# Second weights kept in SBUF for the last 23 single tiles, and the leftover routing cut into one piece a pair

## Chip, cores and metric

The kernel runs on one core of a Trainium2 chip. The metric is the device time of one execution in microseconds; the profiled execution has a span of its own, which is some 2 us shorter than its device time.

## The reference

Cross attention with residual, then a routed feed-forward layer with residual, all in float32. B = 32 samples of 112 rows by 256 (3584 rows), 16 heads of 64, a context of 375 rows by 192 a sample; 8 experts of 256 x 1024 (gate and up) and 512 x 256 (down), two experts a row.

```python
x = x + _L0_xattn_ref(_layernorm(x, axis=-1), ctx_768, Wq, Wkv, Wproj, bproj)
x = x + _L0_ffn_ref(_layernorm(x, axis=-1), gate_w, gate_up_w, down_w)
...
top_k_probs, top_k_idx = jax.lax.top_k(router_probs, TOP_K)
hidden = jax.nn.silu(gate_out) * up_out
expert_out = jnp.einsum('enf,efd->end', hidden, down_w)
output = jnp.sum(sel * top_k_probs[:, :, None], axis=1)
```

Products are made as three passes of split float32 (high by high, high by low, low by high), so each operand has a rounded part (`_h`) and a rest (`_l`).

## The kernel before, in words

The program is one block of five engine programs that meet by semaphores alone. There is no scheduler: each engine runs its instructions in the order in which they are written, and one that waits holds back all behind it on that engine.

**Attention and routing** take the first 1140 us or so, sample by sample. Each row is normalised and written twice, once for each chosen expert, into `bins` in DRAM: 8 experts with a region each, in tiles of 128 rows. The last two samples are routed late, inside the expert stage.

**Expert stage.** There are `NT` = 63 tiles of 128 rows. The first `N1` = 38 are taken as `PAIRS` = 19 pairs, two tiles of one expert that share its weights; the other 25 (tiles 38 to 62) are single tiles, whose rows and experts are known only when the last two samples are routed. `over_tiles` lays out both: before, pairs 0 to 7 written out, a hardware loop (`Fori`) for pairs 8 to 17 (8 to 15 on SP), then pair 18, tiles 38 and 39, a loop over groups of four single tiles, and the last ones written out. `known(p)` is true where p is a plain number, so in written-out code.

A **pair** on TensorE (PE) is 72 products of 256 columns and four transposes: the down product of the pair before, the transposes of the next pair's rows (L1906), the second half of gate and up, and the first half of the next pair's. ScalarE (ACT) and VectorE (DVE) evacuate, split high and low parts (`pairT_h`/`pairT_l`, `hid_h`/`hid_l`), and copy the part of the gate and up weights in use into `still`. The routing of samples B-2 and B-1 is hung on the ends of pair bodies on DVE: `choose`, `mark`, `assign`, then the plan of the single tiles (`tiles_left`, `experts_left`, `rows_left`), which writes `tile_row` and `tile_expert`.

A **single tile** t on PE, between one transpose of rows (L1898) and the next: rows of t+1 turned, the hidden values of t-1 turned (L2016), up of t, gate of t+1, down of t-1. ACT: `hT_h`, `hidT_h`, `silu`, the high part of the down weights of t (L1074), and `y_out` of t-1 (L1082). DVE: `hT_l`, `hidT_l`, `dest_now` and `share_now`, the product of silu and up (L1622, into `in_fours`), the low part of the down weights (L1511). GpSimd (POOL) adds `y_out` into `out` with an indirect DMA (L869); it starts that of t-1 only when that of t-2 has landed, since both can hit one row. SyncE (SP) loads the rows of t+4 (L616) and the down weights of t+2 (L625, 512 KB into one of the two slots of `Wd`), both after the addition of t-1 has landed:

```python
sp.wait_ge(y_store[(k + 1) % 2], 16 * (2 * i + (k - 1) // 2 + 1))
...
load_rows(t + 4, k)
...
load_down(expert_of(t + 2), (k + 1) % 2, "(p k)")
```

With "(p k)" a partition gets four neighbouring rows of the down weights in one run, so the product of silu and up is written in steps of four. With "(k p)" it gets four rows 128 apart.

Of the kernel before, what the change touches and what calls it, by code (L numbers as in the profile page):

```python
# [32 lines left out]
P = 128  # L33
# [26 lines left out]
N2 = NT - N1  # L60

# [127 lines left out]
def over_tiles(eng, pair_of_tiles, tile, end=PAIRS // 2, last=NT // 4):  # L189

    for i in range(4):
        for m in range(2):
            pair_of_tiles(i, m)
    with eng.Fori(4, end) as i:
        for m in range(2):
            pair_of_tiles(i, m)
    for i in range(end, PAIRS // 2):
        for m in range(2):
            pair_of_tiles(i, m)
    pair_of_tiles(PAIRS // 2, 0)  # L200
    for k in (2, 3):
        tile(PAIRS // 2, k)
    with eng.Fori(PAIRS // 2 + 1, last) as i:
        for k in range(4):
            tile(i, k)
    for i in range(last, NT // 4 + 1):
        for k in range(4):
            tile(i, k)
# [12 lines left out]
def attention_and_experts(nc, x, ctx_in, Wq, Wkv, Wproj, bproj, gate_w, gate_up_w, down_w, out):  # L221
# [4 lines left out]
    with ExitStack() as stack:  # L226
# [119 lines left out]
        Wd = sb("Wd", [P, 2, FJ, C], F32)  # L346
# [24 lines left out]
        in_fours = nc.alloc_sbuf_tensor_at("in_fours", [P, FJ, P], F32, offset=still_at)  # L371
# [10 lines left out]
        down_parts = [down_even, sb("down_odd", [P, 2, FJ, C], F32R)]  # L382
# [65 lines left out]
        wd_in = [sem("wd_in0"), sem("wd_in1")]  # L448
# [42 lines left out]
        def _(sp):  # L491
# [131 lines left out]
            def load_down(e, slot, rows="(k p)"):  # L623

                sp.dma_start(Wd[:, slot], down_w[bass.ds(e, 1)].rearrange(f"o {rows} n -> p (o k) n", p=P)).then_inc(wd_in[slot], 16)  # L625

            def pair_of_tiles(i, m):
                p, t = 2 * i + m, 4 * i + 2 * m
                if known(p) and p == 1:
                    sp.wait_ge(x2_done, B)  # L630
                    sp.dma_start(dram_at(tokens, B - 1), x2[:, 1, :]).then_inc(x2_out[1], 16)
                if known(p) and p == PAIRS - 2:
# [10 lines left out]
                if known(p) and p >= PAIRS - 2:  # L643
                    load_down(expert_of(N1 + p - PAIRS + 2), m, "(p k)")
                else:
                    load_down(expert_of(t + 4), m)
# [24 lines left out]
            for p in range(2):  # L671
                load_down(expert_of(2 * p), p)
            over_tiles(sp, pair_of_tiles, tile, PAIRS // 2 - 1, NT // 4 - 1)
# [6 lines left out]
        def _(pool):  # L680
# [181 lines left out]
            norm_h(B - 1, 1, NP - 1)  # L862
# [20 lines left out]
            def pair_of_tiles(i, m):  # L883
# [3 lines left out]
                if known(p) and p == 4:  # L887
                    scatter(B - 2, 0, None)
                if known(p) and p == 7:
# [16 lines left out]
        def _(act):  # L906
# [164 lines left out]
            def hi_of_down(slot, landed):  # L1071

                act.wait_ge(wd_in[slot], 16 * landed)
                nc.scalar.copy(down_parts[slot][:, 0], Wd[:, slot]).then_inc(wd_hi, 1)  # L1074
# [20 lines left out]
            def pair_of_tiles(i, m):  # L1095
# [5 lines left out]
                if there(p - 1, PAIRS):  # L1101
                    for r in range(2):
                        output(t - 2 + r, (2 * m + 2 + r) % 4, pair_down[r], 2 * i + m - 1)
# [4 lines left out]
                hi_of_hidden(p, 0)  # L1108
                silu_of_pair(p, 1)
                if there(p + 1, PAIRS):  # L1110
                    hold_still(e, 1, 0)
                    if not known(p) or p >= 1:
                        act.wait_ge(down_made, t)
                    hi_of_down(1 - m, i + m + 1)
# [9 lines left out]
                if known(p) and p == 4:  # L1124
                    open_gates(B - 1, C_ps)

            def tile(i, k):
# [7 lines left out]
                if there(t, NT):  # L1135
# [6 lines left out]
                    act.wait_ge(down_made, t - 2 if known(t) and t == N1 else t - 1)  # L1142
# [913 lines left out]
```

## Time and profile before

| | us |
|---|---|
| median of 3 runs | 1502.94 (1501.08 to 1502.97) |
| the profiled execution, device time | 1502.86 |
| its span | 1501.1 |
| PE busy | 1424.6 (95%) |
| DVE, ACT, POOL busy | 1060.7, 881.0, 630.0 |
| granted TensorE clock, mean | 0.99 |

The page's table of groups is headed by the attention stage and its share of busy time is an average over all stages. The change is in the last 360 us, so the views below are of that stretch: times in them are counted from the span's start.

### The profile page before, as it was taken

Reading aid. Unit: us, or ns where it says so; the run is one execution under the profiler, and the core shown is the slowest. Engines: PE = TensorE matmul, PEld = TensorE weight load, DVE = VectorE, ACT = ScalarE, POOL = GpSimd, SP = SyncE. Lnnn points to the kernel's source line nnn. Section 1 sums busy time; section 2 is a strip of 40 time slices with the busy share of each in tenths; the row PEclk is TensorE's granted clock in tenths of the full one; section 3 lists DMA queues with packets and bytes.
Section 4 is the critical chain, followed back from the end, with each engine's and each line's share of the span. In section 5 each row is a group of like instructions: output and inputs, shape, how many; then the busy total and the mean of one; then the engine's idle time right before and its main releaser. Section 6 shows DMA issues by size and latency. Waiting matters only on the chain. (4 is left out here: it accounts for less than half of the span.)

```text
span 1501.1 us, 39049 instructions
## 1 busy us (share of the span) xinstructions
PE 1424.6 (95%) x12264; PEld 1272.7 (85%) x12265; DVE 1060.7 (71%) x2906; ACT 881.0 (59%) x2429; POOL 630.0 (42%) x671
## 2 busy tenths in 40 slices
PE   6999999999999999999999999999987999997775
PEld 5888988888888988898888888888877989986664
DVE  5667777777777777777777777777768776654543
ACT  5565655665666665655665665655657767743342
POOL 3634435454435444444544344534373433322222
PEclk9999999999999999999999999999998999999998
DMA  9322222222222222222222232111136555544443
GB/s 269 95 67 69 78 66 74 66 72 72 88 80 89 72 66 73 71 72 69 72 66 79 79 99 78 37 44 33 47 127 218 117 117 120 117 105 115 113 118 85
DMA packets 112077, 134.78 MB, mean 90 GB/s; under 512 B 17980, under 2 KB 95532, under 8 KB 111916
## 3 DMA queue, kind: packets, MB, share of 16 engines
q1 hardware_dynamic: 98860, 115.17, 26.1%
q0 software_dynamic: 12144, 15.66, 5.8%
q10 hardware_dynamic: 1024, 3.34, 0.7%
q8 instruction: 25, 0.41, 0.1%
q14 instruction: 24, 0.20, 0.0%
HBM read 81.16 MB, written 51.93 MB: 89 GB/s over the span
## 5 line engine op out<-in xcount | busy, mean ns | idle before, releaser
L963 ACT ACTIVATE prob<-bank,neg_max 112x375 f32<-112x375 f32 x512 | 300.4, 590 | 133.9 <-DVE neg_max L1429 133.9
L1429 DVE TENSOR_REDUCE neg_max<-bank 112x1 f32<-112x375 f32 x512 | 243.7, 538 | 14.7 <-PE bank L1737 14.6
L1747 PE MATMUL bank<-ident,prob 112*125 112x112 f32 x1536 | 213.8, 273 | 2.7 <-ACT prob L963 2.6
L1747 PEld LDWEIGHTS bank<-ident,prob 112*125 112x125 f32 x1536 | 198.1, 188 | 16.4 <-ACT prob L963 4.8
L869 POOL DMA_INDIRECT out<-y_out,dest_now x63 | 102.1, 1620 | 226.4 <-ACT y_out L1082 202.0
L1771 PEld LDWEIGHTS bank<-probT,V 125*64 125x64 f32 x3072 | 148.1, 137 | 39.1 <-issue 36.4
L1193 DVE TENSOR_TENSOR K_l<-bank,K_h 128x376 fp32r<-128x376 f32 x256 | 140.3, 549 | 56.8 <-ACT K_h L919 52.6
L1771 PE MATMUL bank<-probT,V 125*64 125x112 f32 x3072 | 175.5, 263 | 2.6 <-DVE probT L1435 1.8
L917 ACT COPY V<-bank 125x512 f32<-125x512 f32 x96 | 56.4, 587 | 168.1 <-PE bank L1709 165.5
L919 ACT CAST K_h<-bank 128x376 fp32r<-128x376 f32 x256 | 121.0, 473 | 30.9 <-PE bank L1702 29.3
L798 POOL TENSOR_SCALAR std<-mv 112x1 f32<-112x1 f32 x32 | 7.7, 240 | 283.4 <-DVE mv L1279 283.4
L763 POOL CAST OT_h<-O_now 128x448 fp32r<-128x448 f32 x64 | 37.3, 583 | 209.4 <-DVE O_now L1262 209.4
L969 ACT COPY probT<-bank 125x336 f32<-125x336 f32 x256 | 101.7, 442 | 38.6 <-PE bank L1747 37.7
L1183 DVE COPY V<-bank 125x512 f32<-125x512 f32 x96 | 66.4, 691 | 81.7 <-PE bank L1709 78.7
L1435 DVE COPY probT<-bank 125x336 f32<-125x336 f32 x256 | 123.7, 494 | 0.1
L1645 PE MATMUL bank<-pairT_h,still 128*128 128x256 f32 x608 | 115.6, 286 | 5.8 <-DVE pairT_l L1498 4.2
L1702 PE MATMUL bank<-yA_h,WkH 128*128 128x376 f32 x256 | 99.5, 389 | 12.4 <-DVE WkU L1211 12.4
L963 ACT ACTIVATION_READ_ACCUMULATOR prob<-bank,neg_max 112x1 f32 x512 | 108.4, 212 | 0.0
L1645 PEld LDWEIGHTS bank<-pairT_h,still 128*128 128x128 f32 x608 | 96.3, 191 | 7.2 <-DVE pairT_l L1498 5.2
L1645 PE MATMUL bank<-Wgu,hT_h 128*128 x200 | 68.9, 426 | 32.2 <-DVE hT_l L1504 32.2
L1702 PE MATMUL bank<-WvH,yA_h 128*125 128x512 f32 x192 | 90.9, 474 | 0.0
L921 ACT CAST q_h<-bank 128x224 fp32r<-128x224 f32 x128 | 45.6, 356 | 74.1 <-PE bank L1645 74.1
(244 smaller groups left out, 4128.4 us busy)
## 6 DMA issues: line engine op xcount, KB each, us to landing
bins<-pad_rows SPq DMA_DIRECT2D x29, 1032.0 KB, 5.8
Wd<-in_L_ffn_down_w SPq DMA_DIRECT2D x44, 512.0 KB
inv_rows<-sums SPq DMA_DIRECT2D x126, 128.0 KB, 2.9
h_in<-bins SPq DMA_DIRECT2D x63, 129.0 KB
Wgu<-in_L_ffn_gate_up_w SPq DMA_DIRECT2D x6, 1024.0 KB, 5.6
y_sb<-in_ctx SPq DMA_DIRECT2D x32, 187.5 KB, 2.7
y_sb<-in_ctx SPq DMA_DIRECT2D x62, 93.8 KB, 2.8
x_sb<-in_x SPq DMA_DIRECT2D x16, 224.0 KB, 2.9
```

The costliest lines, as they stand in the source:

```text
L869: pool.indirect_dma_start(out, bass.IndirectOffsetOnAxis(ap=dest_now[:, slot:slot + 1], axis=0), y_out[:, slot % 2, :], None, compute_op=A ...
L919: nc.scalar.copy(K_h[:, arg, :], src[:, 0:LKE]).then_inc(hi_done, 1)
L963: nc.scalar.activation(prob[:, j, :], S_ps[j][0:LQ, 0:LKV], ACT.Exp, bias=neg_max[:, j:j + 1], accum_out=row_sum[:, head // HB, head % HB: ...
L969: nc.scalar.copy(probT[:, j, :], S_ps[j][0:KR, 0:KT * LQ]).then_inc(probT_second, 1)
L1183: nc.vector.tensor_copy(V[:, t, half * 512:half * 512 + 512], src[0:KR, :]).then_inc(v_second, 1)
L1193: nc.vector.tensor_tensor(lo, ps, hi.bitcast(F32), ALU.subtract).then_inc(lo_done, 1)
L1429: nc.vector.tensor_reduce(neg_max[:, j:j + 1], S_ps[j][0:LQ, 0:LKV], AX.X, ALU.max, negate=True).then_inc(max_done, 1)
L1435: nc.vector.tensor_copy(probT[:, j, :], S_ps[j][0:KR, 0:KT * LQ]).then_inc(probT_first, 1)
L1645: last = mm(dst, w, m, start=n == 0, stop=n == len(todo) - 1)
L1702: last = mm(out, w, y, start=begins and n == 0, stop=ends and n == "both")
L1747: last = nc.tensor.transpose(S_ps[j][0:KR, t * LQ:t * LQ + LQ], prob[:, j, t * KR:t * KR + KR], ident[0:LQ, 0:LQ])
L1771: last = mm(O_ps[r * DK:r * DK + DK, c:c + LQ], V[:, t, (2 * p + r) * DK:(2 * p + r) * DK + DK], probT[:, 2 * k + r, t * LQ:t * LQ + LQ], ...
```

## The change

**Single tiles.** From tile 40 (`HELD`) on no down weights are loaded. Four DMAs of 1 MB (`keep_down`) put those of all eight experts into `Wd_all`, which lies over `Wd`, `still` and other tiles of the pair stage; so they are issued only as these come free: experts 0 and 1 in pair 15, 2 and 3 at the start of pair 18's part, 6 and 7 and then 4 and 5 at its end. ACT and DVE read the slice of their tile's expert from `Wd_all` by a register. From load 16 (`LATER`) on, the pairs' weights go to another place, `Wd_later`. SP waits no longer for the addition of t-1, since that wait was there for the slot of `Wd`. The odd slot of the split weights lies elsewhere (`down_third`), and the product of silu and up is written in order.

**Routing.** All 19 pairs are written out. The pieces of the last two samples' routing stand in pairs 1 to 5 and 7 to 12 instead of 1 to 7, each with less in it.

**Order in a pair.** ACT makes `y_out` of the second tile two steps later; DVE copies `dest_now` and `share_now` after the low parts. The residual of the last sample and the first split of down weights stand in the middle of pair 0, and POOL normalises the last sample after the first additions.

```diff
+LATER = 16
+HELD = N1 + 2
...
+        Wd_later = nc.alloc_sbuf_tensor_at("Wd_later", [P, 2, FJ, C], F32, offset=plan2_at)
+        Wd_all = nc.alloc_sbuf_tensor_at("Wd_all", [P, E, FJ, C], F32, offset=wd_at)
...
+            def keep_down(first):
+
+                sp.dma_start(Wd_all[:, first:first + 2].rearrange("p e k n -> p (e k) n"),
+                             down_w[first:first + 2].rearrange("e (k p) n -> p (e k) n", p=P)).then_inc(wd_all, 16)
...
+                if p == PAIRS - 1:
+                    sp.wait_ge(up_made, 2 * PAIRS - 1)
+                    keep_down(2)
                 sp.wait_ge(hT_made, t + 2)
                 sp.wait_ge(dest_done, t + 2)
...
+                load_down(p + 2, t + 4 if p + 2 < PAIRS else N1 + p + 2 - PAIRS)
+                if p == LATER - 1:
+                    sp.wait_ge(wd_lo, LATER)
+                    keep_down(0)
+                if p == PAIRS - 1:
+                    sp.wait_ge(down_made, 2 * PAIRS - 2)
+                    keep_down(6)
+                    sp.wait_ge(up_made, 2 * PAIRS)
+                    keep_down(4)
...
             def tile(i, k):
                 t = 4 * i + k
-                if there(t + 2, NT):
-                    sp.wait_ge(y_store[(k + 1) % 2], 16 * (2 * i + (k - 1) // 2 + 1))
-                    sp.sem_inc(passed, 1)
                 if there(t + 4, NT):
                     sp.wait_ge(hT_made, t + 1)
                     sp.wait_ge(dest_done, t + 1)
                     sp.sem_inc(passed, 1)
                     load_rows(t + 4, k)
-                if there(t + 2, NT):
-                    sp.wait_ge(wd_lo, t + 1 - PAIRS)
-                    sp.sem_inc(passed, 1)
-                    load_down(expert_of(t + 2), (k + 1) % 2, "(p k)")
...
-                    act.wait_ge(down_made, t - 2 if known(t) and t == N1 else t - 1)
-                    hi_of_down((k + 1) % 2, 2 * i + (k - PAIRS) // 2 + 1)
...
+                if there(t, NT):
+                    act.wait_ge(down_made, N1 if known(t) and t < HELD else t - 1)
+                    if known(t) and t < HELD:
+                        hi_of_down(t - PAIRS, down_parts[k % 2])
+                    else:
+                        if known(t) and t == HELD:
+                            act.wait_ge(wd_all, 64)
+                        nc.scalar.copy(down_parts[k % 2][:, 0], Wd_all[:, expert_of(t)]).then_inc(wd_hi, 1)
...
+                    nc.vector.tensor_tensor(silu[:], up_ps[k % 2][:], silu[:], ALU.mult).then_inc(hid_done, 1)
...
-                if known(p) and p == 1:
+                if p == 1:
                     choose(B - 2)
+                if p == 2:
                     mark(B - 2, 0)
-                if known(p) and p == 2:
+                if p == 3:
                     assign(B - 2, 0)
```

On ACT, one single tile of the loop, before:

```order
L1069 CAST hT_h<-bank 128x256
L1132 REGISTER_ALU
L1134 CAST hidT_h<-bank 128x512
L1141 ACTIVATE silu<-bank 128x512
L1073 ISA
L1074 CAST down_even<-Wd 128x1024
L1080 REGISTER_ALU
L1082 ACTIVATE y_out<-bank,share_now 128x256
```

and with the change:

```order
L1077 CAST hT_h<-bank 128x256
L1142 REGISTER_ALU
L1144 CAST hidT_h<-bank 128x512
L1151 ACTIVATE silu<-bank 128x512
L1095 ISA
L1095 TENSOR_LOAD tile_expert
L1095 ISA x2
L1162 ISA
L1162 COPY down_third<-Wd_all 128x1024
L1089 REGISTER_ALU
L1091 ACTIVATE y_out<-bank,share_now 128x256
```

The cast of the down weights stands where it stood, and a register load of the expert's number has come in ahead of it; its source is no longer filled by a DMA of this tile.

On SP, one single tile of the loop, before (the rows of t+4, then the weights of t+2):

```order
L614 ISA
L614 TENSOR_LOAD tile_row
L614 ISA x2
L616 ISA
L616 DMA h_in<-bins 128x258
L659 REGISTER_ALU
L620 REGISTER_ALU
L620 TENSOR_LOAD tile_expert
L620 ISA x2
L625 ISA
L625 DMA Wd<-in_L_ffn_down_w 128x1024
```

and with the change:

```order
L614 ISA
L614 TENSOR_LOAD tile_row
L614 ISA x2
L616 ISA
L616 DMA h_in<-bins 128x258
```

Of two loads a tile one is left, the 129 KB of rows.

On DVE, the end of pair 1 and the start of pair 2, before (the three rows at the top are the end of `mark`):

```order
L1337 TENSOR_SCALAR hn<-top,inv_top 112x2
L1340 COPY hn<-dest 112x2
L1341 TENSOR_SCALAR dest<-dest 112x2
L1550 TENSOR_LOAD tile_expert
L1550 ISA x2
L1557 ISA
L1557 COPY still<-Wgu 128x512
L1518 CAST dest_now<-h_in 128x1
L1519 COPY share_now<-h_in 128x1
L1518 CAST dest_now<-h_in 128x1
L1519 COPY share_now<-h_in 128x1
L1498 TENSOR_TENSOR pairT_l_158<-bank,pairT_h_156 128x512
```

and with the change:

```order
L1532 TENSOR_TENSOR down_even<-Wd_first,down_even 128x1024
L1337 MAX top<-gates 112x8
L1340 MAX_INDEX top_i<-top,gates 112x8
L1570 TENSOR_LOAD tile_expert
L1570 ISA x2
L1577 ISA
L1577 COPY still<-Wgu 128x512
L1518 TENSOR_TENSOR pairT_l_160<-bank,pairT_h_158 128x512
L1564 TENSOR_TENSOR hid_l<-silu,hid_h 128x512
L1538 CAST dest_now<-h_in 128x1
L1539 COPY share_now<-h_in 128x1
L1538 CAST dest_now<-h_in 128x1
```

Only `choose` (two instructions) is left at the end of pair 1, `mark` has gone to pair 2, and `pairT_l`, for which PE waits, stands ahead of the four small copies.

## Rows read from the trace of the kernel before

**Rows 1.** Windows of the expert stage: length, busy (count) by engine, PEclk, DMA share, GB/s.

```profile
1147.45:1235.73 88.28, 83.23 (x697) 81.98 (x696) 68.57 (x188) 63.60 (x113) 34.99 (x24) 1.00 0.52 113
1235.73:1316.47 80.74, 80.74 (x687) 80.74 (x685) 55.72 (x130) 61.78 (x107) 30.11 (x18) 1.00 0.56 119
1336.87:1474.36 137.49, 106.03 (x603) 87.66 (x602) 65.53 (x120) 53.43 (x100) 30.94 (x20) 0.98 0.48 117
```

**Rows 2.** Timeline, PE: the transposes that begin tiles 39, 41 and 61.

```profile
1326.95 0.38 PE L1898 MATMUL bank<-ident,h_in 128*128 128x128 f32 x2
...
1336.87 0.38 PE L1898 MATMUL bank<-ident,h_in 128*128 128x128 f32 x2
...
1474.36 0.38 PE L1898 MATMUL bank<-ident,h_in 128*128 128x128 f32 x2
```

**Rows 3.** Chain that ended last, 1402 to 1417: start, us, what.

```profile
1402.86 5.38 DMA out<-y_out,dest_now
...
1410.59 3.81 DMA Wd<-in_L_ffn_down_w
...
1415.38 0.47 ACT y_out L1082
...
1416.66 5.19 DMA out<-y_out,dest_now
```

**Rows 4.** Line 869: landing of additions begun in 1340-1450, 1200-1250 and 1250-1300.

```profile
DMA to landing us min/median/max: 5.2/5.3/5.6
...
DMA to landing us min/median/max: 3.7/3.8/4.2
...
DMA to landing us min/median/max: 4.0/4.4/4.5
```

**Rows 5.** Timeline, POOL: the additions of pair 18's second tile and of tile 38.

```profile
1328.87 1.55 POOL L869 DMA_INDIRECT out<-y_out,dest_now  x1 [0.30 <-issue]
1333.76 1.55 POOL L869 DMA_INDIRECT out<-y_out,dest_now  x1 [3.34 <-DMA out<-y_out,dest_now]
```

**Rows 6.** Groups by form: busy, mean ns; 1340-1480, the last row 1235-1316.

```profile
L1622 DVE TENSOR_TENSOR in_fours<-bank,silu 128x512 f32<-128x512 f32 x21 | 22.5, 1072 | 0.0
...
L1511 DVE TENSOR_TENSOR down_odd<-Wd,down_odd 128x1024 fp32r<-128x1024 f32 x11 | 13.5, 1225 | 40.9 <-ACT down_odd L1074 40.9
...
L1074 ACT CAST down_odd<-Wd 128x1024 fp32r<-128x1024 f32 x10 | 10.5, 1048 | 42.1 <-DMA Wd<-in_L_ffn_down_w 42.1
...
L1539 DVE TENSOR_TENSOR silu<-bank,silu 128x512 f32<-128x512 f32 x9 | 6.2, 692 | 6.9 <-PE bank L1645 6.9
```

**Rows 7.** Timeline of the end, PE, ACT and POOL.

```profile
1480.87 0.60 PE L2016 MATMUL bank<-ident,in_fours 128*128 128x128 f32 x4
...
1483.13 0.51 PE L1645 MATMUL bank<-down_even,hidT_h 128*128 128x256 f32 x2 [0.26 <-DVE hidT_l L1614]
...
1484.66 0.60 PE L2016 MATMUL bank<-ident,in_fours 128*128 128x128 f32 x4
...
1490.32 0.79 PE L1645 MATMUL bank<-down_odd,hidT_h 128*128 128x256 f32 x2 [5.06 <-DVE hidT_l L1614]
...
1493.29 0.47 ACT L1082 ACTIVATE y_out<-bank,share_now 128x256 f32<-128x256 f32 x1 [4.03 <-PE bank L1645]
1494.58 1.55 POOL L869 DMA_INDIRECT out<-y_out,dest_now  x1 [3.43 <-ACT y_out L1082]
```

**Rows 8.** Waits of PE in 1147 to 1235, the longest; in 1340 to 1474, both.

```profile
PE bank L1645 <- DVE pairT_l L1498: 4.2, 5, 1.8
...
PE bank L1645 <- DVE hT_l L1504: 30.9, 19, 2.6
PE bank L1898 <- issue: 0.5, 2, 0.3
```

**Rows 9.** Timeline, PE: down product of pair 17 begins; one window of a weight load.

```profile
1313.59 0.40 PE L1645 MATMUL bank<-down_odd,hid_h 128*128 128x256 f32 x2
...
1322.00:1323.00 1.00, 1.00 (x6) 0.81 (x5) 0.33 (x1) 1.00 (x2) 0.00 (x0) 1.00 1.09 317
```

More of the change, by code:

```diff
@@ L186, in over_pairs, with over_tiles @@
         body(NP)
[L189 to L200, printed above, removed]
+def over_tiles(eng, pair_of_tiles, tile):
+    for p in range(PAIRS):
+        pair_of_tiles(p // 2, p % 2)
     for k in (2, 3):
         tile(PAIRS // 2, k)
-    with eng.Fori(PAIRS // 2 + 1, last) as i:
+    for k in range(4):
+        tile(PAIRS // 2 + 1, k)
+    with eng.Fori(PAIRS // 2 + 2, NT // 4 - 1) as i:
         for k in range(4):
             tile(i, k)
-    for i in range(last, NT // 4 + 1):
+    for i in range(NT // 4 - 1, NT // 4 + 1):
         for k in range(4):
@@ L671, in _ @@
             for p in range(2):
-                load_down(expert_of(2 * p), p)
-            over_tiles(sp, pair_of_tiles, tile, PAIRS // 2 - 1, NT // 4 - 1)
+                load_down(p, 2 * p)
+            over_tiles(sp, pair_of_tiles, tile)
             for k in range(2):
@@ L886, in pair_of_tiles @@
                     add_pair(p - 1, 1 - m)
-                if known(p) and p == 4:
+                if p == 1:
+                    norm_h(B - 1, 1, NP - 1)
+                if p == 5:
                     scatter(B - 2, 0, None)
-                if known(p) and p == 7:
+                if p == 11:
                     scatter(B - 1, 1, None)
@@ L1108, in pair_of_tiles @@
                 hi_of_hidden(p, 0)
+                if there(p - 1, PAIRS):
+                    output(t - 1, (2 * m + 3) % 4, pair_down[1], p - 1)
                 silu_of_pair(p, 1)
@@ L1123, in pair_of_tiles @@
                     hold_still(e, 0, 0)
-                if known(p) and p == 4:
+                if p == 6:
                     open_gates(B - 1, C_ps)
@@ L1146, in tile @@
                         output(t - 2 + r, (k + 2 + r) % 4, pair_down[r], PAIRS - 1)
-                elif there(t - 1, NT):
+                if there(t, NT):
[6 more added lines that the diff above has]
+                        nc.scalar.copy(down_parts[k % 2][:, 0], Wd_all[:, expert_of(t)]).then_inc(wd_hi, 1)
+                if there(t - 1, NT) and not (known(t) and t == N1):
                     output(t - 1, (k + 3) % 4, down_ps, 2 * i + (k - 1) // 2)
@@ L1571, in pair_of_tiles @@
                 lo_of_hidden(p, 0)
+                for r in range(2):
+                    keep_dest(t + r, p - 1, 2 * m + r)
+                if p == 0:
+                    residual(NP, B - 1, 1, C_ps)
+                    lo_of_down(0, down_even)
                 if there(p + 1, PAIRS):
@@ L1621, in tile @@
                     dve.wait_ge(up_made, t + 1)
-                    nc.vector.tensor_tensor(in_fours[:].rearrange("p j n -> p n j"),
-                                            up_ps[k % 2][:].rearrange("p (n j) -> p n j", j=FJ),
-                                            silu[:].rearrange("p (n j) -> p n j", j=FJ), ALU.mult).then_inc(hid_done, 1)
-                    lo_of_down(t - PAIRS, (k + 1) % 2)
+                    nc.vector.tensor_tensor(silu[:], up_ps[k % 2][:], silu[:], ALU.mult).then_inc(hid_done, 1)
+                    if known(t) and t < HELD:
+                        lo_of_down(t - PAIRS, down_parts[k % 2])
+                    else:
+                        dve.wait_ge(wd_hi, t - PAIRS + 1)
+                        nc.vector.tensor_tensor(down_parts[k % 2][:, 1], Wd_all[:, expert_of(t)],
+                                                down_parts[k % 2][:, 0].bitcast(F32), ALU.subtract).then_inc(wd_lo, 1)
             e = expert_of(0)
@@ L2015, in tile @@
                     for j in range(FJ):
-                        last = nc.tensor.transpose(hidT_ps[:, j * P:j * P + P], in_fours[:, j, :], ident[:])
+                        last = nc.tensor.transpose(hidT_ps[:, j * P:j * P + P], silu[:, j * P:j * P + P], ident[:])
                     last.then_inc(hidT_made, 1)
```

82 lines of the change are left out of this document (41 added, 41 removed).

## The prediction

> **What bounds the kernel now.** I read the windows first, to see in which stretches TensorE (PE) is not at work. From pair 10's transposes to the end of the pairs it is busy 80.74 of 80.74 us, 9 pairs of 8.97 us: there PE bounds, and nothing on another engine is worth anything. Over the nine pairs ahead of these it is busy 83.23 of 88.28 us. Over the 20 single tiles from 41 on it is busy 106.03 of 137.49 us at 117 GB/s [rows 1]. So most of what can be had lies in the single tiles: 137.49 / 20 = 6.87 us each.
>
> Then the timeline, for what a tile costs when nothing holds it. Tiles 39 and 40 ran on weights loaded during the pairs, and take 1336.87 - 1326.95 = 9.92 us, 4.96 each [rows 2]. The other 1.9 us of a tile are waits, and PE's list of waits names them: 30.9 us for `hT_l` of DVE, 19 times [rows 8]. DVE is not the cause. Its cast of the down weights sat idle 40.9 us for ACT's, and ACT's 42.1 us for the DMA of the weights (each for one of the two slots) [rows 6]. `hT_l` stands behind them on DVE.
>
> The chain of waits says what those weights wait for: addition of `y_out` begun at 1402.86, landed after 5.38; SP loads the rows, then at 1410.59 the weights; 3.81 us; cast, `y_out` at 1415.38, next addition at 1416.66 [rows 3]. That ring of 13.8 us turns once in two tiles, since there are two slots, so 6.9 us a tile: it is what sets the pace of the 20 tiles.
>
> **The change part by part.** All sums are against the profiled execution, 1502.86 us of device time with a span of 1501.1; the median is 1502.94, so what is taken off the one comes off the other. A change of 0.2% is 3 us, about what a measurement of this kernel can tell.
>
> *Single tiles.* The load of weights and the wait for the addition leave the ring. What limits next?
> - PE: 4.96 us a tile [rows 2]. The hardware loop over four tiles also showed 0.5 us without a releaser at two of its turns [rows 8]. I take 5.0; the upper bound from PE is its busy time in the 20 tiles, 5.3 each [rows 1], which holds the slow restarts behind each wait.
> - ACT and DVE: busy 53.43 / 20 = 2.7 and 65.53 / 20 = 3.3 us a tile [rows 1]. The product of silu and up without the stride should take what the same form takes in the pairs, 0.69 instead of 1.07 [rows 6]: less work for DVE. Each gets a register load of the expert. SP's pair of such a load and its issue sits within the 2.3 us between landing (1408.24) and the issue of the weights at 1410.59, which also holds another load and an issue, so it is under 1.2 us [rows 3]. With that ACT has under 3.9 and DVE under 4.2, both under 5.0. Hidden by PE; uncovered from 1.1 us more on.
> - POOL: additions stay one after the other. Where an addition waited only for the one before, it began at 1333.76, behind one begun at 1328.87 [rows 5]: 4.9 us from start to start, landing included. The landing itself took 5.2 to 5.6 us in the single tiles, but 3.7 to 4.2 and 4.0 to 4.5 in two stretches of the pairs [rows 4]. There the 512 KB of weights are begun later than the first addition of a pair; in the single tiles they are begun 1 us behind it. With them gone I take 4.0, between the low stretch and the high one; with the 0.9 us from landing to the next start that is 4.9, a hair under PE's 5.0.
>
> Saved: 137.49 - 20 x 5.0 = 37.5 us.
>
> *The end.* Tile 61 took 1480.87 - 1474.36 = 6.51 [rows 2, 7]; 5.0 saves 1.5. From the last transposes (1484.66) to the last down product (1490.32) it was 5.66 us, with a wait of 5.06 behind the weights; one tile before the same steps took 1483.13 - 1480.87 = 2.26 [rows 7]. Saves 3.4. The last down product took 1493.29 - 1490.32 = 2.97 at PE's lower clock level, against 1484.66 - 1483.13 = 1.53 [rows 7]; with a shorter gap ahead of it I take the latter. Saves 1.4. Sum 6.3 us.
>
> *Routing and the order in a pair.* Of the 88.28 us of the nine early pairs, 9 x 8.97 = 80.74 would be the pace of the late ones: 7.5 us too much, 5.05 of them idle and the rest products of the routing and the clock, which stay. Idle is mostly the wait for `pairT_l`, 4.2 us in five, the longest 1.8 [rows 1, 8]; it comes where a long piece of routing stands ahead of `pairT_l` on DVE. The pieces get shorter, but `mark` and `rows_left` are kept whole, and the copies behind `pairT_l` now take only 0.3 off. Bounds: 0 (same waits at other pairs) and 5. I take the middle, 2.5.
>
> *The burst.* Experts 2, 3, 6, 7, 4, 5, the rows of two tiles and one pair's 512 KB, 3.8 MB, go out from 1313.59 (the first half of pair 18 is done) [rows 9]. ACT waits for all four DMAs at tile 40. Its body begins at 1331.9; with `y_out` of tile 39 and `hT_h` of tile 42 behind the cast on ACT, PE feels a delay from about 1336.5 on: 23 us. At the 317 GB/s of a full window [rows 9] the bytes take 12 us, at 512 KB in 3.81 [rows 3], each on its own, 28. So 0 to 5 us; nearer to the first, since DMAs overlap. But the additions of pair 18 fall into the burst, and start the chain of additions late, by some 2 to 4 us, with little room to catch up (4.9 against 5.0). I take 1.2 us lost. The 1 MB of pair 15 goes out in a stretch that is at 56% of its DMA time [rows 1]: nothing.
>
> Sum: 37.5 + 6.3 + 2.5 - 1.2 = 45.1; 1502.86 - 45.1 = 1457.8. I say **1458**.
>
> **The rivals.**
> - *Additions become the bound.* The landing could be long in the single tiles for what stays there, the rows' load or the pace, not for the weights. At 5.3 [rows 4] and 0.9, a tile takes 6.2: from tile 38's addition at 1333.76, 24 more end the chain at 1482.6 instead of 1494.58 [rows 5, 7], 12.0 us; with the pairs and the burst, 13.3: 1490. Against it: the landings of the pairs, each with two loads of rows beside them. Chance 0.1. At 4.4, the middle of the higher stretch, it is 5.3 a tile: 1333.76 + 127.2 = 1461.0, 33.6 saved, 34.9 in all: 1468. Chance 0.15.
> - The Trainium skill (DMA: Bandwidth & Descriptors, section on the anatomy of one DMA) says that a DMA's fixed part of about 2 us is mostly the receipt of its last write, which the time of other transfers would not touch. Were all of the 5.3 such a receipt, that would speak for the first of these; the rows of one and the same 128 KB addition between 3.7 and 5.6 us speak against. Its fit gives 2.3 us for 128 KB, an estimate under every row here; by it the sum stays as it is, since PE bounds.
> - *Slower: the written-out pairs starve the engines of instructions.* Ten pairs (8 to 17) leave the loop, and PE's program grows by a third. To outweigh 45 us it needs 4.5 us a pair. The early pairs are written out already, and all their idle time, 5.05 us in nine, is named: 4.2 for `pairT_l` and most of the rest for `hid_l` [rows 1, 8]. At under 0.1 us each it is under 1 us for ten: 1459. Chance of slower 0.02.
> - The Trainium skill (Runtime: NRT & Kernel Launch, section on instruction fetch) goes the other way: a taken branch breaks the prefetch, so written-out code should gain. In the loop's stretch PE had no idle time at all [rows 1], so I count nothing.
> - *The change does nothing here* (another link keeps the ring at 6.9): 1500 to 1503. With the weights resident no row leads there. 0.02.
>
> **How the numbers follow.** PE bounds: 0.71, 1451 to 1464, from period 4.9 (-2), pairs 5 (-2.5), no loss in the burst (-1.2), against pairs 0, burst 5, and period 5.1. Better than that 0.01 (rounding of the rest). Additions at 5.3 us a tile: 0.15, 1464 to 1473. Additions at 6.2: 0.10, 1484 to 1493. No change or slower: 0.04. 1450 to 1474 holds 0.8 of it, after a little for what I did not see. Faster 0.96, same 0.02, slower 0.02.
>
> **What would show it.** In the new profile: PE's transposes L1898's successors 4.9 to 5.1 us apart from tile 41 on; landings of single-tile additions about 4.0; no wait of ACT on a DMA but at tile 40; POOL's idle time ended by `y_out`, not by the addition before (if by the latter, additions bound); PE's waits for `pairT_l` in pairs 1 to 12 about half of 4.2 us; the last down product within 2.3 us of the last transposes. The prediction is wrong if landings stay over 4.4, if the wait for `Wd_all` at tile 40 exceeds 5 us, or if DVE or ACT need over 5 us a tile with the register loads.

## The result, and the profile after

The changed kernel takes 1456.37 us (1455.95 to 1457.93, 4 runs), the kernel before beside it 1502.07 (1501.08 to 1502.97): ratio 0.9698, 95% interval 0.9681 to 0.9715. Predicted were 1458, in 1450 to 1474. The ratios below leave out two executions of the run without resident weights, of 1488.68 us and, at a granted clock of 0.752, of 1715.71 us. The profiled execution has a span of 1454.6 us against 1501.1: 46.5 us less.

Windows of the changed kernel, in the columns of [rows 1]: from the transposes of pair 0's rows to those of tile 38's rows; from there to tile 42's rows; the same 20 tiles as the third row of [rows 1]; and the end.

```profile
1138.10:1312.02 173.92, 169.97 (x1407) 167.99 (x1407) 131.08 (x317) 128.88 (x226) 63.78 (x42) 0.98 0.59 129
1312.02:1334.49 22.47, 20.96 (x133) 18.12 (x131) 11.18 (x27) 10.20 (x19) 8.54 (x5) 1.00 0.86 234
1334.49:1432.55 98.06, 98.06 (x602) 86.97 (x601) 62.34 (x120) 53.59 (x100) 30.84 (x20) 1.00 0.31 50
1432.55:1454.60 22.05, 10.73 (x70) 9.12 (x68) 6.46 (x10) 6.66 (x12) 6.17 (x4) 0.86 0.24 30
```

The same stretches of the kernel before:

```profile
1140.05:1316.47 176.42, 169.79 (x1408) 168.16 (x1407) 131.59 (x322) 131.54 (x227) 65.11 (x42) 0.98 0.55 122
1316.47:1336.87 20.40, 20.40 (x133) 18.23 (x131) 10.89 (x24) 9.25 (x18) 7.80 (x5) 1.00 0.43 82
1474.36:1501.10 26.74, 12.21 (x70) 10.19 (x68) 7.90 (x11) 7.46 (x13) 6.19 (x4) 0.76 0.30 66
```

The account of the 46.5 us comes from these: 2.5 saved in the pairs, 2.1 lost between them and the single tiles, 137.49 - 98.06 = 39.4 saved in the 20 tiles, 4.7 saved at the end. The rest, 1140.05 - 1138.10 = 1.95 us, lies in the attention stage. It is scatter and no gain: over all profiles of this case pair 0's transposes begin between 1136.8 and 1146.0 us, in no order with the edits. The 2.5 us of the pairs are more than scatter: that stretch takes 175.9 to 176.4 us in the three profiles with the old pairs, and 173.5 to 174.0 in the eight with the new pairs and an unchanged start. In the 20 tiles PE is now busy all the time, 4.90 us a tile, where it was busy 77% of it.

PE's waits in 1138 to 1455 of the changed kernel say what is left of [rows 8], in the same columns:

```profile
PE bank L1674 <- DVE hid_l L1564: 2.0, 2, 1.5
PE bank L1674 <- DVE pairT_l L1518: 1.7, 2, 1.4
PE bank L1674 <- DVE hidT_l L1641: 1.4, 1, 1.4
PE bank L1674 <- DVE hT_l L1524: 1.3, 2, 1.1
PE bank L2045 <- DVE silu L1649: 0.2, 1, 0.2
```

The 30.9 us for `hT_l` are 1.3. The landing of the additions, from the instances of line 875 in 1340 to 1430, stands against the first row of [rows 4]; behind it a late addition from the timeline:

```profile
DMA to landing us min/median/max: 3.7/3.9/4.4
...
1434.68 1.54 POOL L875 DMA_INDIRECT out<-y_out,dest_now  x1 [2.99 <-DMA out<-y_out,dest_now]
```

They land after 3.9 us instead of 5.3. Nine of the 18 in this stretch start only as the one before lands (the others are released by `y_out` or by DVE's copy), and PE still never waits: the chain of additions runs a hair faster than PE's 4.90.

### The profile page after: what moved, and what is told of

Read it like the earlier page. It is cut to its first block and busy times, and to the rows that moved or that the text cites. A ratio compares the mean times of both kernels' runs of the same rounds, so it can differ in the third digit from the quotient of the medians.

```text
span 1454.6 us, 38552 instructions
## 1 busy us (share of the span) xinstructions
PE 1413.2 (97%) x12264; PEld 1270.6 (87%) x12265; DVE 1057.0 (73%) x2905; ACT 879.4 (60%) x2428; POOL 628.2 (43%) x671
## 5 line engine op out<-in xcount | busy, mean ns | idle before, releaser
L1766 PE MATMUL bank<-K_h,q_h 64*112 64x376 f32 x512 | 88.4, 342 | 0.0
```

Of the source, the lines that this page charges most:

```text
L1766: last = mm(S_ps[2 * k + r][0:LQ, 0:LKE], w[rows, p, q], m[rows, p, :], start=n == 0, stop=n == len(todo) - 1)
```

## The experiments

Absolute times shift by some us between sessions, so only ratios to the kernel before, measured beside each, are compared. "Rows of tile 38" is the transposes of that tile's rows.

**Is it the ring?** The kernel before without SyncE's wait for the landed addition in single tiles; `wd_lo` alone guards the slot of the weights.

```diff
-                if there(t + 2, NT):
-                    sp.wait_ge(y_store[(k + 1) % 2], 16 * (2 * i + (k - 1) // 2 + 1))
-                    sp.sem_inc(passed, 1)
```

> The kernel before with one edit: in a single tile SP no longer waits for the addition of t-1 ahead of the rows of t+4 and the weights of t+2 (the slots are still guarded by the waits on wd_lo, hT_made and dest_done). All loads of weights stay. Theory: two things made a tile 6.87 us, the ring (addition, then load) and the weight load beside the addition, which makes the landing 5.3 instead of 4.0 us. The edit opens the ring alone, so additions bound, 5.3 + 0.9 = 6.2 us a tile: 1489 to 1492 us. Rival, only the ring mattered: 4.9 to 5.0 us a tile, about 1462 us, and the resident weights bring nothing of their own.

Measured: ratio 0.9711 (0.9695 to 0.9727). Three lines gone give nearly the whole gain, with the same 512 KB still loaded for every tile. Its stretch from tile 38's rows to tile 42's, its 20 tiles, and two tiles of its timeline, SyncE and POOL:

```profile
1319.15:1345.67 26.52, 22.71 (x133) 20.01 (x131) 11.80 (x25) 10.19 (x19) 8.89 (x5) 0.87 0.49 110
1345.67:1443.41 97.74, 97.74 (x603) 86.86 (x601) 66.76 (x120) 53.53 (x100) 30.95 (x20) 1.00 0.64 158
```
```profile
1380.35 0.34 SPq L625 DMA_DIRECT2D Wd<-in_L_ffn_down_w  x1
...
1381.65 1.55 POOL L866 DMA_INDIRECT out<-y_out,dest_now  x1 [3.30 <-DMA out<-y_out,dest_now]
...
1385.45 0.35 SPq L625 DMA_DIRECT2D Wd<-in_L_ffn_down_w  x1
1386.46 1.55 POOL L866 DMA_INDIRECT out<-y_out,dest_now  x1 [3.26 <-DMA out<-y_out,dest_now]
```

In the 20 tiles DMA works twice as much as in the changed kernel (0.64 against 0.31), and PE never waits. What this run loses lies ahead of them, 26.52 us against 20.40: there a load fell 1.28 us behind the start of an addition of 1.76 us, and the next came after 8.07. But the rows also show why the run doesn't refute contention: with the wait gone, the load went out 1.0 to 1.5 us *ahead* of an addition (1.3 and 1.0 in the rows shown), and not 0.5 to 1.0 us behind it as before. Two things had changed at once.

**The wait or the loads, in the changed kernel.** First loads that nobody reads, then the wait alone.

```diff
+                    sp.wait_ge(wd_lo, t + 1 - PAIRS)
...
+                    sp.dma_start(Wd_later[:, k % 2], down_w[0:1].rearrange("o (p k) n -> p (o k) n", p=P))...
```

> The changed kernel with one addition: from tile 40 on SP loads 512 KB of down weights a tile into the dead slots of Wd_later, which nobody reads and nobody waits for but the next load into the same slot. Same ring as after, same traffic as before. Theory of contention: landings of the additions go from about 3.9 to 5.3 us and POOL's chain sets the pace, 6.2 us a tile, 25 us more than after: about 1481 us. Rival, no contention: 1456 to 1458 us.

```diff
+                    sp.wait_ge(y_store[(k + 1) % 2], 16 * (2 * i + (k - 1) // 2 + 1))
```

> The changed kernel with SP's wait for the addition of t-1 put back ahead of the rows of t+4. Rows are needed three tiles later and the landing of 2.6 us fits, so: no change from after, within 0.2%, 1456 to 1458 us. Rival, the wait itself holds the stage: rows late, some 1 us a tile or more, 1475 us and over.

Measured: 0.9705 (0.9692 to 0.9718) and 0.9698 (0.9684 to 0.9712). Neither costs anything that these ratios can tell. The loads again stood 1.2 to 1.9 us ahead of most additions.

**Loads put beside the addition.** An unread load of 512 KB again, now behind `y_done` of the tile. It isn't quite the same load: it takes the tile's expert and "(k p)", so pieces of 1 KB a row instead of 4 KB.

```diff
-                    sp.wait_ge(wd_lo, t + 1 - PAIRS)
+                    sp.wait_ge(y_done, t)
...
-                    sp.dma_start(Wd_later[:, k % 2], down_w[0:1].rearrange("o (p k) n -> p (o k) n", p=P))...
+                    sp.dma_start(Wd_later[:, k % 2], down_w[bass.ds(expert_of(t), 1)].rearrange("o (k p) n -> p (o k) n", p=P))...
```

> The changed kernel with a load of 512 KB of down weights in every single tile from 40 on that nobody reads, issued when the output rows of a tile are ready, so together with the start of their addition. In the kernel before such a load was issued 0.96 us behind the start of an addition (1403.82 against 1402.86), and the additions took 5.2 to 5.6 us to land; in the run with unread loads issued 1.3 us ahead of the addition they took 4.0. Theory of contention: a load that is issued within about 1 us of the addition's start makes it land after 5.3 us or more; additions follow one another at 5.3 + 0.9 = 6.2 us, and bound: 20 tiles take 124 us instead of 98, the time is about 26 us longer than the changed kernel's, 0.987 of before. Rival: the weights' transfer costs the addition nothing wherever it is put, the landing is about 4.0, tiles stay 4.9 apart, ratio 0.970.

Measured: 0.9732 (0.9715 to 0.9750); the unchanged kernel in the same session 0.9707 (0.9691 to 0.9722):

> The changed kernel once more, beside the others of this call, so that they can be compared with it in one session. Ratio to the kernel before 0.970 (first measured 0.9698, 0.9681 to 0.9715); its single tiles 4.90 us apart, and 20 to 25 us from tile 38's transposes to tile 42's.

The intended place was missed. POOL starts an addition only when the last has landed, so the load, behind `y_out` alone, still went out 1.1 to 1.9 us ahead of most. Landing 4.1 us in the middle, 20 tiles in 98.06. Of the 4 us lost against the unchanged kernel, 3.1 are in the end (1460.2 - 1435.36 = 24.8 against 1453.8 - 1432.04 = 21.8, from the start of tile 61 to the end of the span), in which one of POOL's instructions took 2.04 us; one shortly ahead of it took 1.89.

So the wait and the load were both put back where they had been in SyncE's program, with nobody reading the load:

```diff
+                if there(t + 2, NT):
+                    sp.wait_ge(y_store[(k + 1) % 2], 16 * (2 * i + (k - 1) // 2 + 1))
...
                 if there(t + 4, NT):
...
                     load_rows(t + 4, k)
...
+                    sp.dma_start(Wd_later[:, k % 2], down_w[bass.ds(expert_of(t), 1)].rearrange("o (k p) n -> p (o k) n", p=P))...
```

> The changed kernel with SyncE's wait for the landed addition put back ahead of the rows' load, and behind both an unread load of 512 KB of down weights in each single tile from 40 on, so at the place in SyncE's program that it had before. An addition starts 0.9 us after the last has landed, so such a load should be issued some 1 to 2 us behind an addition's start, while in the two runs with unread loads so far it was issued 1.3 to 1.6 us ahead of one. Nothing reads the load, so there is no ring. Theory of contention by position: in the run without resident weights, additions with a load issued 1.9 to 2.1 us behind their start came 7.2 to 7.6 us before the next, those with one at 2.3 us or more, or ahead of it, 4.6 to 4.9; so here additions follow one another at 6 us or more for as long as the loads stay in that place, the 20 tiles take 120 us or more, and the time is 20 us or more longer than the changed kernel's: ratio 0.983 or more. Rival, that position means nothing and the long landings of before belong to the ring: 4.9 a tile, ratio 0.970 to 0.973.

Measured: 0.9746 (0.9728 to 0.9763). Its 20 tiles, PE's waits in them, and POOL and SyncE at two places:

```profile
1340.04:1442.77 102.73, 99.05 (x603) 86.97 (x601) 62.58 (x120) 54.70 (x101) 30.84 (x20) 1.00 0.63 143
```
```profile
PE bank L1937 <- DMA h_in<-bins: 3.6, 4, 1.2
```
```profile
1346.44 1.54 POOL L885 DMA_INDIRECT out<-y_out,dest_now  x1 [3.36 <-ACT y_out L1101]
...
1347.28 0.39 SPq L677 DMA_DIRECT2D Wd_later<-in_L_ffn_down_w  x1
...
1352.90 1.54 POOL L885 DMA_INDIRECT out<-y_out,dest_now  x1 [4.92 <-DVE share_now L1549]
...
1388.77 1.54 POOL L885 DMA_INDIRECT out<-y_out,dest_now  x1 [3.54 <-DMA out<-y_out,dest_now]
...
1390.28 0.39 SPq L677 DMA_DIRECT2D Wd_later<-in_L_ffn_down_w  x1
...
1393.36 1.54 POOL L885 DMA_INDIRECT out<-y_out,dest_now  x1 [3.05 <-DMA out<-y_out,dest_now]
```

The addition at 1346.44 had its load 0.84 us behind its start, and the next addition came 6.46 us later; the one at 1388.77 had it 1.51 us behind (POOL's instruction was nearly over), and the next came after 4.59. Most loads fell at 1.4 to 1.5, where the next came after 4.6 to 5.2, but once after 6.3. So the price was 4.7 us in 20 tiles, not the 22 or more expected: the sign was right, the size more than four times too big. Position matters, and within some tenths of a us.

PE's waits name the path: 3.6 us, all for rows. A late addition holds SyncE's wait, and the wait holds the load of rows. That fits the two runs above, where the wait without loads and the loads without the wait cost nothing.

This run is the nearest to the kernel before in which no tile waits for the load: 102.73 us against 137.49. **Of the 39.4 us, 34.8 lie between the kernel before and this run, 4.7 between this run and the changed kernel.** The first is not the price of the ring alone, since the load differs in two ways: in the kernel before it fell 0.5 to 1.0 us behind nearly every addition, here mostly 1.2 to 1.5, and here it comes in pieces of 1 KB. The landings of 5.3 instead of 3.9 us were a part of the ring: they are 1.4 us longer, once a turn, and the 20 tiles are ten turns, so by estimate 14 of the 34.8 us need both, the ring and the load beside the addition. How much the ring would cost with short landings no run shows.

**What is residence worth then?** The changed kernel with the weights loaded anew for each single tile, no wait and nothing resident:

```diff
+                    sp.dma_start(Wd_later[:, (k + 1) % 2], down_w[bass.ds(expert_of(t + 2), 1)].rearrange("o (k p) n -> p (o k) n", p=P))...
...
-                            act.wait_ge(wd_all, 64)
-                        nc.scalar.copy(down_parts[k % 2][:, 0], Wd_all[:, expert_of(t)])
+                        act.wait_ge(wd_in[(k + 1) % 2], 16 * (2 * i + (k - PAIRS) // 2 + 1))
+                        nc.scalar.copy(down_parts[k % 2][:, 0], Wd_later[:, (k + 1) % 2])
```

> The changed kernel with the down weights loaded anew for each single tile, two tiles ahead, into two slots, as before, but without the wait for an addition, and without the loads that keep all experts' weights: so the change without its headline. If residence itself is worth nothing once the wait is gone: ratio 0.970, tiles 4.9 apart. If it is worth what the run of the kernel before without the wait lacked (0.9711 against 0.9698), ratio 0.971, and from tile 38's transposes to tile 42's 24 to 27 us as in that run (26.5), since loads of weights then fall beside the last additions of the pairs.

Measured: 0.9805 (0.9761 to 0.9848), so 0.9805 - 0.9707 = 1.0% or 15 us slower than the changed kernel, and unsteady: the times behind the ratio spread over 19 us, from 1464.27 to 1483.72, those of the changed kernel over 5. Both expectations missed it. Its POOL, DVE and SyncE in a slow stretch and in a fast one, and an addition near the end, behind the last load:

```profile
1342.90 1.22 DVE L1647 TENSOR_TENSOR down_even<-Wd_later,down_even 128x1024 fp32r<-128x1024 f32 x1
1343.02 2.51 POOL L869 DMA_INDIRECT out<-y_out,dest_now  x1 [5.14 <-ACT y_out L1085]
...
1344.91 0.39 SPq L661 DMA_DIRECT2D Wd_later<-in_L_ffn_down_w  x1
...
1350.60 2.51 POOL L869 DMA_INDIRECT out<-y_out,dest_now  x1 [5.07 <-ACT y_out L1085]
...
1369.91 1.54 POOL L869 DMA_INDIRECT out<-y_out,dest_now  x1 [3.06 <-DVE share_now L1532]
...
1374.52 1.54 POOL L869 DMA_INDIRECT out<-y_out,dest_now  x1 [3.07 <-DMA out<-y_out,dest_now]
...
1451.26 2.51 POOL L869 DMA_INDIRECT out<-y_out,dest_now  x1 [4.94 <-ACT y_out L1085]
```
```profile
DMA to landing us min/median/max: 6.4/6.7/6.7
...
DMA to landing us min/median/max: 3.7/3.8/4.1
```

The landings are those of 1340 to 1360 and of 1365 to 1420. In the slow stretch POOL begins its addition 0.12 us behind the start of DVE's 1.22 us subtraction and takes 2.51 instead of 1.54; the load goes out within it; it lands after 6.7; and since `y_out` and `dest_now` wait for landings, the next round falls into the same place, 7.6 us a tile. (The profile puts POOL's idle time down to `y_out`; the landing at about 1349.7, 0.9 us ahead of the start at 1350.60, fits as well.) It leaves this step after four additions and falls into it again at 1429. Without a load beside it, the long instruction alone costs less: the addition at 1451.26 was followed after 5.57 us.

So residence is worth 1.0% against this run, and 0.1% or less, within the intervals, against the first one, the kernel before without the wait. What keeps that one out of the slow step isn't shown. Its product of silu and up takes 1.1 us instead of 0.7, so DVE's subtraction comes later behind a landing, and its loads are in pieces of 4 KB; neither was tried by itself. Nor does the load alone bring the step on: the runs with unread loads, in pieces of 4 KB and of 1 KB, took 97.70 and 98.06 us for their 20 tiles.

**The loads at the end of the pairs.** The last four experts not loaded, and each tile from 40 on computed with expert 2's weights:

```diff
-                if p == PAIRS - 1:
-                    sp.wait_ge(down_made, 2 * PAIRS - 2)
-                    keep_down(6)
-                    sp.wait_ge(up_made, 2 * PAIRS)
-                    keep_down(4)
...
-                        nc.scalar.copy(down_parts[k % 2][:, 0], Wd_all[:, expert_of(t)])
+                        nc.scalar.copy(down_parts[k % 2][:, 0], Wd_all[:, 2])
```

> The changed kernel without the loads of the last four experts' weights (4, 5, 6, 7: two of the three transfers, 2 MB, issued at the end of the pairs), and with every single tile from 40 on taking expert 2's weights. Theory A, the burst of transfers delays the additions and the landing of rows at the end of the pairs: from tile 38's transposes to tile 42's 20.0 instead of 22.5 us, 1 to 2.5 us faster than the changed kernel. Theory B, it is the place of the high part of the down weights on ScalarE behind the outputs of pair 18, which stays: 22 to 22.5 us and the same time within 1 us.

Measured: 0.9702 (0.9682 to 0.9721), against 0.9707. From tile 38's rows to tile 42's 21.72 us, against 22.42 in the unchanged kernel of that session. The step from tile 40's rows to tile 41's stayed, 6.28 us against 6.25, so theory B has most of it. The changed kernel's own rows, ACT, DVE, POOL, PE:

```profile
1323.15 0.47 ACT L1091 ACTIVATE y_out<-bank,share_now 128x256 f32<-128x256 f32 x1 [0.95 <-PE bank L1674]
1323.52 1.04 ACT L1083 CAST down_even<-Wd_later 128x1024 fp32r<-128x1024 f32 x1
...
1324.59 1.22 DVE L1532 TENSOR_TENSOR down_even<-Wd_later,down_even 128x1024 fp32r<-128x1024 f32 x1 [4.87 <-ACT down_even L1083]
1325.73 0.42 DVE L1524 TENSOR_TENSOR hT_l<-bank,hT_h 128x256 fp32r<-128x256 f32 x1
...
1324.86 2.37 POOL L875 DMA_INDIRECT out<-y_out,dest_now  x1 [0.30 <-issue]
...
1326.29 0.73 PE L1674 MATMUL bank<-Wgu,hT_h 128*128 x2 [1.12 <-DVE hT_l L1524]
```

Tile 38's weights now go to `down_even`, as pair 18's do, and are written in ACT's program behind pair 18's two outputs. DVE waits 4.87 for the cast, `hT_l` stands behind its subtraction, and PE waits 1.12. With the smaller burst the same rows read 4.94 and 1.13, and the addition that meets the subtraction takes 2.37 in both. That this order costs the rest is read from the rows; no run moved the cast back. What the burst did is in the same stretch: the next `dest_now` waits 2.13 us for the pair's first addition, begun at 1323.01 and landed 5.9 us later. With the smaller burst that wait is gone.

**Routing pieces, and the order within a pair.** Each undone by itself in the changed kernel: the old larger pieces (`choose` and `mark` in pair 1, and so on), and the old order (both outputs on ACT, and both copies of destinations on DVE, first). Of each diff a part is shown.

```diff
                     choose(B - 2)
-                if p == 2:
                     mark(B - 2, 0)
```

> The changed kernel with the pieces of the last two samples' routing put back to pairs 1 to 7 as before (still written out, order in a pair as changed). Compared with after, theory: the stretch from the first pair's transposes to tile 38's (169.0 us before, 166.7 after) gets back most of the 2.3 us, so 1457.5 to 1459 us. Rival, the gain there is of the order within a pair: no change from after.

```diff
+                for r in range(2):
+                    keep_dest(t + r, p - 1, 2 * m + r)
                 if there(p + 1, PAIRS):
                     lo_of_pair(p + 1, m)
```

> The changed kernel with the order in a pair as before: ACT makes both y_out ahead of the next pair's high part, DVE copies dest_now and share_now ahead of pairT_l. Compared with after, theory: up to 0.3 us for each pair in which PE waits for pairT_l or hid_l, under 1.5 us in all: 1456 to 1458 us. Rival, this order carries the 2.3 us of the pairs: 1458.5 us or more.

Measured: 0.9710 (0.9697 to 0.9723) and 0.9708 (0.9691 to 0.9725), and the pairs' stretch:

```profile
1140.71:1314.74 174.03, 168.59 (x1408) 166.35 (x1407) 130.71 (x317) 129.01 (x226) 63.80 (x42) 0.99 0.58 129
```
```profile
1144.60:1318.25 173.65, 168.26 (x1408) 166.35 (x1407) 131.28 (x321) 131.24 (x226) 63.09 (x42) 1.00 0.59 132
```

Against 173.92 and 176.42: either half alone keeps the gain, though PE's idle time in that stretch is 5.4 us with either, against 6.6 before and 4.0 in the changed kernel; PE's busy time makes up for it. The timeline of the kernel before shows what stands ahead of `pairT_l` at one of PE's two long waits for it, 1.63 of the 4.2 us:

```profile
1169.46 0.15 DVE L1518 CAST dest_now<-h_in 128x1 int32<-128x1 f32 x1 [1.01 <-DMA out<-y_out,dest_now]
1169.51 0.47 ACT L1082 ACTIVATE y_out<-bank,share_now 128x256 f32<-128x256 f32 x1 [1.26 <-DMA out<-y_out,dest_now]
...
1169.88 0.58 ACT L1036 CAST pairT_h<-bank 128x512 fp32r<-128x512 f32 x1
...
1170.49 0.69 DVE L1498 TENSOR_TENSOR pairT_l<-bank,pairT_h 128x512 fp32r<-128x512 f32 x1 [0.81 <-ACT pairT_h L1036]
```

ACT's second `y_out` waited 1.26 us for an addition to land, with `pairT_h` behind it, and `pairT_l` waited 0.81 for `pairT_h`. DVE stood 1.01 us for the same landing, at a copy of 0.15 us, with `pairT_l` behind it. The new order takes both from ahead of the pair's parts. The longest wait, 1.76 us at 1230.08, has no landing in it: there DVE waited 1.37 us for PE at a copy into `still`, and the four small copies and `pairT_l` came behind. Why the old order with the new pieces takes no longer isn't explained: with it PE waits 2.8 us for `pairT_l`, less than the 4.2 before and more than the 1.7 with the whole change.

**Other parts.** The kernel before with its loop of pairs written out (SyncE's too), and the changed kernel with the last sample's `OT_h`, `OT_l` made by ACT and DVE in place of POOL, for which PE waits.

```diff
-    with eng.Fori(4, end) as i:
+    for i in range(4, end):
```

> The kernel before with its 19 pairs written out and nothing else changed. Theory: the loop cost nothing, as PE had no idle time in it: 1501 to 1503 us. Rival of starved instruction fetch: slower by 1 us or more a pair for ten pairs, over 1510. Rival that a taken branch costs: faster by over 3 us.

```diff
-            split_O(2 * B - 1, 1, B - 1)
+            act.wait_ge(O_done, 2 * B)
...
+            nc.scalar.copy(OT_h[:, HALF:2 * HALF, :]..., O_now[:]).then_inc(OT_hi, 1)
...
+            dve.wait_ge(OT_hi, 2 * B)
+            nc.vector.tensor_tensor(OT_l[:, HALF:2 * HALF, :]..., O_now[:], hi.bitcast(F32), ALU.subtract)...
```

> The changed kernel with one more change, tried as a version that may beat both: the last half of the attention output (O_now of the last sample) is split by ACT (high part) and DVE (low part) instead of POOL, whose two instructions took 2.5 and 3.1 us there beside DVE's splits of expert weights, with PE idle for 5.8 us behind them. Theory: PE's projection starts 4 us earlier, but the first pair then waits for pairT_l behind the same splits on DVE, so 0.5 to 2 us faster: about 1455 us. If the clock of PE stays at its higher level there, up to 4 us. Rival: DVE's chain only gets longer by 0.6 us: 1457 us.

Measured: 0.9973 (0.9963 to 0.9984), 4 us faster where the theory expected nothing. That is the size which the rival of the taken branch gave, but no row shows branches as the cause. The pairs, where the edit is, take 175.88 us against 176.42 in the profile of the kernel before (176.12 in the run without the wait, which has the loop); the end from tile 61 on, which the edit leaves alone, is 1.4 us shorter. The rest is open. And 0.9710 (0.9697 to 0.9723), no gain: the first wait shrinks, and the rows' load is late next. PE of the changed kernel, then of this one:

```profile
1135.40 0.56 PE L1821 MATMUL bank<-WpH,OT_h 128*112 128x256 f32 x1 [5.77 <-POOL OT_l L772]
```
```profile
1134.33 0.37 PE L1827 MATMUL bank<-WpH,OT_h 128*112 128x256 f32 x1 [1.19 <-DVE OT_l L1548]
1140.54 1.24 PE L1941 MATMUL bank<-ident,h_in 128*128 128x128 f32 x4 [4.54 <-DMA h_in<-bins]
```

## Why the prediction was right, and where not

- **The sum is nearer than its terms.** They missed by +1.9 (single tiles), -1.6 (end), 0 (pairs) and -0.9 us (burst), 0.6 in all, so 44.5 us saved against 45.1. That 1458 came within 2 us of 1456.4 is in part luck. Two sums of the prediction don't come out: its case of PE as the bound adds up to 1452 to 1466, not 1451 to 1464, and its chances to 1.01.
- **Single tiles: 37.5 predicted, 39.4 measured.** The ring was the cause, and PE bounds next, as said. The term was 0.1 us a tile too careful (5.0 for 4.90): the hardware loop shows no wait at its turns any more.
- **ACT and DVE hidden**: right. The product of silu and up takes 0.69, the register load shows at tile 40 as 0.61 us of DVE idle ahead of its subtraction, and the two are busy 2.7 and 3.1 us a tile.
- **Landing 4.0**: 3.9. The reason given, loads that begin close behind the addition, holds (the run with wait and loads put back shows it), but only for loads issued while POOL is still at the addition. Three runs whose loads stood ahead of it showed no long landing in the 20 tiles. One of the prediction's signs was too strict, that additions bound if POOL's idle time is ended by the addition before: it is so in 9 of 18, and PE doesn't wait.
- **What the ring needed**: the prediction ascribed its end to the residence. Taking out the wait alone opened it; without the wait the loads fit under PE. Nor was the wait needed for the slot of `Wd`, as is said where the change is described: `wd_lo` guards that slot, in the kernel before too. What the prediction didn't see is that without the wait *and* with loads there can be a second, slow step, which the run without resident weights fell into. In the profiles with resident weights at most two long instructions of POOL follow one another.
- **The end: 6.3 predicted, 4.7 measured.** PE's part came out: from the start of tile 61 to the last output 12.2 us instead of 18.9 (its last wait is 1.40, not 5.06). The term left out the chain of additions. The last output begins at 1444.73; in [rows 7] an addition follows its output by 1.29 us, which gives 1446.0; it began at 1448.27, since the four ahead ran landing to start:

```profile
1434.68 3.84 DMA out<-y_out,dest_now
1439.40 3.47 DMA out<-y_out,dest_now
1443.74 3.66 DMA out<-y_out,dest_now
```

  (the chain of waits of the changed kernel; start, us). That is 2.2 us. The near tie of 4.9 against 5.0 was named in the prediction, but not carried to the end of the kernel.
- **Pairs: 2.5 predicted, 2.5 measured**, but not by its step. "A long piece of routing stands ahead of `pairT_l`" is half of it: in a wait of 1.63 us ACT stood 1.26 at a landing ahead of `pairT_h`, and the longest, 1.76, had neither ahead of it. Either half of the edit keeps the gain. `pairT_l` still takes 1.7 of PE's time, against 4.2.
- **The loads at the end of the pairs: 1.2 predicted, 2.1 measured**, and again by another step. ACT doesn't wait for the transfers at tile 40. Without 2 MB of them 0.7 is won, since an addition of pair 18 lands late in the burst, as the prediction said. The rest goes, as far as the rows tell, to the place of tile 38's cast, which the prediction didn't cost though its order was there to be read.
- **Rivals.** Additions as the bound, at 5.3 or 6.2 us a tile: not here; but this is what the run with wait and loads put back does at single additions, and the run without residence for stretches. Slower through written-out pairs: the opposite sign, 0.9973. The prediction counted nothing for a gain there; 4 of the 45.7 us may be one.

## What to carry to other kernels

When a wait closes a ring (store lands, load goes out, cast, compute, store), first ask whether the wait guards anything; here three lines gave nearly what the resident weights gave. Moving or removing a wait also moves the transfer behind it, so read each transfer's start against its neighbours' before calling contention shown or refuted. And compare the spread of two versions, not only their medians: the one with loads and no wait was fast only while its engines happened not to meet.

## What the runs showed of the hardware

- POOL's indirect addition takes 1.54 us, and 2.57 down to 1.76 where it begins 0.06 to 0.87 us behind the start of DVE's 1.22 us subtraction of two SBUF tensors: what is left of DVE's instruction, less some 0.12 us, is added. Where it began ahead of it, at most 0.04 us behind its start, or at its end, it took 1.54; nor did the 1.1 us product that reads one operand from PSUM lengthen it (1.55 at 0.20 us behind its start). The Trainium skill (SBUF — State Buffer, two separate sides) says that the two engines share one port pair, an exclusive lock held for the whole instruction, which DVE takes with two SBUF inputs against a GpSimd instruction that reads SBUF; where DVE is first the trace agrees (2.51 - 1.54 = 0.97, with 1.10 of DVE's 1.22 left). Where POOL was first it doesn't show DVE blocked: subtractions that began 0.3 to 0.9 us into POOL's 1.54 took 1.22 to 1.23 us, as ever.
- The same 128 KB addition lands after 3.5 to 6.7 us. With POOL's instruction at 1.54 us, 85 additions of the single tiles had their 512 KB loads 1.0 us or more ahead of their start, or 1.4 or more behind it; the next addition came after 4.5 to 5.5 us, with five exceptions of up to 6.8. With the load 0.3 and 0.8 us behind, in the run with wait and loads put back, it came after 6.05 and 6.46. Counted from the end of POOL's instruction the long ones fall together too: a load issued 2.06 us behind the start cost nothing where the instruction took 1.54 (next after 4.68), and one at 2.07 was followed after 7.17 where it took 2.57. Long were those with the load 0.5 to 1.2 us ahead of that end, and one at 0.2. Why the place matters so sharply is open.
- With the waits gone, PE's busy time for the same 20 tiles fell from 106.03 to 98.06 us, 8.0 us of the 39.4. The granted clock is a part of it. Of the kernel before, the first four tiles and the other sixteen:

```profile
1336.87:1365.18 28.31, 23.09 (x122) 19.25 (x121) 13.22 (x24) 10.77 (x20) 6.19 (x4) 0.88 0.49 117
1365.18:1474.36 109.18, 82.94 (x483) 68.40 (x482) 52.31 (x96) 42.66 (x80) 24.76 (x16) 1.00 0.48 117
```

  At 4.90 us a tile, 3.5 us of the 8.0 are in the four tiles at 0.88 and 4.5 in the sixteen at 1.00, with PE busy 5.18 us a tile. What the 4.5 are isn't shown; the profile models the ends of products, and one with nothing behind it may count for longer.
